# The clip of the scores in an integer softmax, moved from VectorE to GpSimd

## The chip, the cores and the metric

The kernel runs on one core of a Trainium2 chip. The metric is the device time of one execution in microseconds. The engines of the core are TensorE (PE in the profile; PEld is its weight load), VectorE (DVE), ScalarE (ACT), GpSimd (POOL) and SyncE (SP), which here only issues DMAs.

## The reference

The reference is a tower of eight blocks over tokens of 192 features: a choice of 87 of 125 tokens in each of 32 samples, then attention and feed-forward blocks in turn. The change lies in one of them, the attention of the third layer. Its 12 heads have 16 features each; queries, keys and values are quantised to whole numbers between -128 and 127, and the softmax is done on whole numbers:

```python
attn = jnp.einsum('bhnd,bhmd->bhnm', q, k) * Dh ** (-0.5)
attn = fq_act(attn, s_attn)            # round(t / s), clipped to 8 bits
...
x_int = x / scale
x_int = x_int - jnp.max(x_int, axis=-1, keepdims=True)
x_int = jnp.maximum(x_int, n * x0_int)
q = jnp.floor(x_int / x0_int)
r = x_int - x0_int * q
z = r * (r + b_int) + c_int
exp_int = jnp.maximum(jnp.floor(z * jnp.exp2(n - q)), 0.0)
exp_sum = jnp.sum(exp_int, axis=-1, keepdims=True)
ratio = jnp.round(exp_sum / jnp.maximum(exp_int, 1.0))
big = jnp.floor(jnp.log2(ratio))       # and a correction; out = 2 ** -big
```

## The kernel before, in words

The stage is `log_int_stage`. The 32 samples are taken two at a time: 16 units, j = 0 to 15. A unit has 2 x 12 heads x 87 queries as rows, packed into 17 chunks of 128 partitions, each chunk with 87 keys. In SBUF a chunk has a pitch of 88 columns, so a tile is 128 x 1496. Each engine has its own written-out order, with semaphores that count units between them. All tiles of the stage (`raw`, `score`, `above`, `lift`, `e`, `share` and so on) exist once, so each engine also waits until a tile has been read before it writes it for the next unit.

The steps of one unit, with the lines that the profile shows:

- `scores` (TensorE, L2418, L2424): q times k into PSUM `ps`. The query blocks come by DMAs that SP issues (L2452) after `scores_done` of an earlier unit.
- `take` (ScalarE, L3306, L3307): `ps` to `raw`, int32, rounded. It waits for `cut` of the unit before, since `raw` exists once.
- `clip` (VectorE, L3380): `raw` to `score`, bf16, clipped to -128 to 127. It waits for `raw_ready` of its unit and `less_done` of the unit before.
- `find_top` (VectorE, L3385, L3387, L3390): the maximum of each row, in two halvings and a reduction, to `top`.
- `take_off_top` (TensorE, L3253, L3255): score minus top in PSUM `mid`, by an identity and a minus identity. It waits for `top_ready` and for `squared` of the unit before, since `mid` exists once; its end is `less_done`.
- `lift_up` (ScalarE, L3311): `mid` to `above`, bf16.
- `quotient` (VectorE, L3365): `above` to `lift`, bf16.
- `remainder` (TensorE, L3264), `powers` (ScalarE, L3330), `squares` (ScalarE, L3334, ends in `squared`).
- `exponential` (VectorE, L3357, `e` from `square` and `power`), `sum_up` (L3361), `divide` (L3369, L3371, L3373, `share` from `e` and the reciprocals).
- `lines` (ScalarE, L3326, from `share`), `exponents` (VectorE, L3394 `sure`, L3399 `classes`).
- `turn` (TensorE, L3272), `copy_turned` (ScalarE, L3319, L3321), `weigh` (TensorE, L2758), `store` (VectorE, L3403).

These are overlapped across units. In one round j, VectorE does exponential j, sum_up j, quotient j+1, divide j, clip j+2, find_top j+2, exponents j, store j-1. ScalarE does lift_up j+1, copy_turned j-1, lines j, powers j+1, squares j+1, take j+3. TensorE does take_off_top j+1, turn j-1, remainder j+1, weigh j-1, scores j+3. GpSimd does only the memsets at the start of the stage (L3227, L3228).

Of the kernel before, what the change touches and what calls it, by code (L numbers as in the profile page):

```python
# [16 lines left out]
ALU = mybir.AluOpType  # L17
# [57 lines left out]
def across(ap, axis, n):  # L75

    ap = ap.unsqueeze(axis)
    shape = list(ap.shape)
    shape[axis] = n
    return ap.broadcast_to(shape)  # L80
# [3096 lines left out]
def chunks_of(sb):  # L3177

    return sb[:].rearrange("r (n k) -> r n k", k=PITCH)


def log_int_stage(kit, QK, VB, out, con, heads):
# [6 lines left out]
    nc = kit.nc  # L3189
    s_qk, ninv_x0, bound, whole_x0, half_b, rest_c, sigma = (con[:, j:j + 1] for j in (0, 3, 11, 12, 13, 14, 4))  # L3190
    to_int = con[0:NT, 15:16]
    U = UNITS
# [3 lines left out]
    with kit.stage("log_int") as ctx:  # L3196
        blocks, filled = heads.of, heads.filled
        raw, power, line, sure = (kit.sb(ctx, n, [128, FLAT], I32) for n in ("raw", "power", "line", "sure"))
        square, e, share = (kit.sb(ctx, n, [128, FLAT]) for n in ("square", "e", "share"))
        score, above, lift, classes = (kit.sb(ctx, n, [128, FLAT], BF16) for n in ("score", "above", "lift", "classes"))  # L3200
# [23 lines left out]
        @block.gpsimd  # L3224
        def _(pool):
            for k, value in enumerate((2.0 ** 21, 128.0 * (LEAST + CLASS0))):
                nc.gpsimd.memset(bias[:, k:k + 1], value).then_inc(made, 1)  # L3227
            nc.gpsimd.memset(raw[:], -1024).then_inc(made, 1)  # L3228

        @block.sync  # L3230
        def _(sp):
# [118 lines left out]
        @block.vector  # L3350
        def _(dve):
            v = nc.vector

            def exponential(j):
                dve.wait_ge(squared, j + 1)
                dve.wait_ge(power_ready, j + 1)
                v.scalar_tensor_tensor(e[:], square[:], rest_c, power[:].bitcast(F32), ALU.add, ALU.mult).then_inc(e_ready, 1)  # L3357

            def sum_up(j):
                dve.wait_ge(e_ready, j + 1)  # L3360
                v.tensor_reduce(total[:], chunks_of(e)[:, :, 0:NT], AX.X, ALU.add).then_inc(summed, 1)  # L3361

            def quotient(j):
                dve.wait_ge(above_ready, j + 1)
                v.tensor_scalar(lift[:], above[:], ninv_x0, whole_x0, ALU.mult, ALU.add).then_inc(lift_ready, 1)  # L3365

            def divide(j):
                dve.wait_ge(summed, j + 1)
                v.tensor_scalar(total[:], total[:], 1.0, None, ALU.max).then_inc(floored, 1)  # L3369
                dve.wait_ge(floored, j + 1)  # L3370
                v.reciprocal(recip[:], total[:]).then_inc(recip_ready, 1)  # L3371
                dve.wait_ge(recip_ready, j + 1)
                v.scalar_tensor_tensor(chunks_of(share), chunks_of(e), NEAR, across(recip[:], 2, PITCH), ALU.mult,  # L3373
                                       ALU.mult).then_inc(share_ready, 1)

            def clip(j):
                dve.wait_ge(raw_ready, j + 1)
                if j >= 1:
                    dve.wait_ge(less_done, j)
                v.tensor_scalar(score[:], raw[:], -128.0, 127.0, ALU.max, ALU.min).then_inc(cut, 1)  # L3380

            def find_top(j):
                dve.wait_ge(cut, j + 1)
                of = chunks_of(score)
                v.tensor_tensor(half[:], of[:, :, 0:PITCH // 2], of[:, :, PITCH // 2:PITCH], ALU.max).then_inc(halved, 1)  # L3385
                dve.wait_ge(halved, j + 1)
                v.tensor_tensor(quarter[:], half[:, :, 0:PITCH // 4], half[:, :, PITCH // 4:PITCH // 2],  # L3387
                                ALU.max).then_inc(quartered, 1)
                dve.wait_ge(quartered, j + 1)
                v.tensor_reduce(top[:], quarter[:], AX.X, ALU.max).then_inc(top_ready, 1)  # L3390

            def exponents(j):
                dve.wait_ge(line_ready, j + 1)
                v.tensor_tensor(sure[:], share[:].bitcast(I32), line[:], ALU.add).then_inc(sure_ready, 1)  # L3394
                dve.wait_ge(sure_ready, j + 1)
                if j >= 1:
                    dve.wait_ge(turned_done, j)
                high = sure[:].bitcast(I16).rearrange("r (w half) -> r w half", half=2)[:, :, 1]
                v.tensor_scalar(classes[:], high, -1.0 / 128.0, 254.75 - 1.0 / 256.0, ALU.mult, ALU.add).then_inc(class_ready, 1)  # L3399

            def store(j):
                dve.wait_ge(weighed, j + 1)
                v.tensor_scalar(out[:, 2 * j:2 * j + 2, :], p_out[:, :, 0:D], to_int, MAGIC, ALU.mult, ALU.add).then_inc(stored, 1)  # L3403

            v.memset(ps[:], 0.0).then_inc(cleared, 1)
            v.tensor_scalar(minus[:], kit.identb[:], -1.0, None, ALU.mult).then_inc(cleared, 1)
            v.tensor_scalar(times_x0[:], kit.identb[:], sigma, None, ALU.mult).then_inc(cleared, 1)
            for j in range(-AHEAD, U + 1):
                if has(j):
                    exponential(j)  # L3410
                    sum_up(j)
                if has(j + 1):
                    quotient(j + 1)
                if has(j):
                    divide(j)
                if has(j + 2):
                    clip(j + 2)
                    find_top(j + 2)
                if has(j):
                    exponents(j)  # L3420
                if has(j - 1):
                    store(j - 1)
# [231 lines left out]
def l2_attn(kit, H, stats, early, loads):  # L3654
    nc, dram = kit.nc, kit.dram
    W3 = 3 * D
    with ExitStack() as outer:
# [7 lines left out]

        CX = sb("cx", [NT, NB, D])
        log_int_stage(kit, QKB, VB, CX, con, heads)
        with ExitStack() as last:
            CT = sb("cT", [KP, HALVES, TOKENS], BF16, last)
# [127 lines left out]
```

## Time and profile before

| | |
|---|---|
| median of 3 runs | 2383.24 us (2379.29 to 2392.43) |
| time of the profiled execution | 2381.72 us |
| its span | 2379.3 us |
| busy in the span: PE, DVE, ACT, POOL | 1676.9, 1323.9, 1044.3, 344.1 us |
| the stage, from the first clip to the last store | 1431 to 1635 us |
| mean granted clock of TensorE, as a share of full speed | 0.83 |

The profile is one execution. Times in its rows are us from the start of the span unless they are marked ns. A row of the timeline has a start, a duration, engine, line, operation, written tile, read tiles, sizes, and in brackets the idle time of the engine before it with what ended it. Consecutive instructions of one form can be merged in one row ("x2").

### The profile page before, as it was taken

The numbers are of one execution on the slowest core, as the hardware profiler recorded it, in microseconds if no ns is written. First come the engines' busy times: TensorE is split into PE (matmuls) and PEld (weight loads), VectorE is DVE, ScalarE is ACT, GpSimd is POOL, SyncE is SP. The second block draws the span as 40 slices with busy tenths as digits, with TensorE's granted clock in tenths as the row PEclk, the third lists the DMA queues.
The fourth block names the chain that finished last, engine by engine and source line by source line (L and its number), as shares of the span: only waits on it lengthen the run. The fifth ranks groups of instructions, "written<-read, shape, count | busy, mean of one in ns | idle before, by whom it ended". The sixth has DMA issues, their size and how long they took to land. (4 is left out here: it accounts for less than half of the span.)

```text
span 2379.3 us, 35751 instructions
## 1 busy us (share of the span) xinstructions
PE 1676.9 (70%) x12022; PEld 1359.0 (57%) x12038; DVE 1323.9 (56%) x2732; ACT 1044.3 (44%) x2115; POOL 344.1 (14%) x417
## 2 busy tenths in 40 slices
PE   3588879947751377656589686664793699469995
PEld 2266658636641244336579563443683598369995
DVE  6599962350147989978712467997326211542223
ACT  4477742302224678876112147884322254312221
POOL 0000000006630000001043100000000342034431
PEclk9799969877875588987689896775897699679998
DMA  3200010304440000000467300000003453446775
GB/s 85 69 19 18 21 26 4 83 24 136 138 157 1 4 6 6 5 1 2 124 215 215 125 4 8 7 4 1 13 1 109 141 181 116 138 133 223 225 215 190
DMA packets 137245, 189.81 MB, mean 80 GB/s; under 512 B 51661, under 2 KB 111214, under 8 KB 137070
## 3 DMA queue, kind: packets, MB, share of 16 engines
q1 hardware_dynamic: 116289, 146.91, 20.2%
q0 software_dynamic: 15360, 36.72, 5.3%
q10 hardware_dynamic: 5420, 3.91, 0.6%
q8 instruction: 102, 1.67, 0.3%
q14 instruction: 74, 0.60, 0.1%
HBM read 150.21 MB, written 33.68 MB: 77 GB/s over the span
## 5 line engine op out<-in xcount | busy, mean ns | idle before, releaser
L989 DVE TENSOR_TENSOR 36_l3f_mlp_hidden<-36_l3f_mlp_gate,36_l3f_mlp_first 128x512 f32<-128x512 f32 x51 | 35.1, 688 | 185.3 <-ACT 36_l3f_mlp_gate L967 104.6
L882 PE MATMUL 36_l3f_mlp_first<-36_l3f_mlp_xT,36_l3f_mlp_w 128*128 128x128 f32 x816 | 101.5, 278 | 1.9 <-issue 1.9
L1005 DVE TENSOR_SCALAR 9_l0f_mlp_y<-9_l0f_mlp_second,l0f_routing_weight 128x192 f32<-128x192 f32 x51 | 20.4, 416 | 142.7 <-PE 9_l0f_mlp_second L896 63.1
L882 PEld LDWEIGHTS 36_l3f_mlp_first<-36_l3f_mlp_xT,36_l3f_mlp_w 128*128 128x128 f32 x816 | 97.0, 195 | 1.6 <-issue 1.6
L1245 PE MATMUL 2_performer_p_u<-perf_proj,2_performer_yT 128*87 128x512 f32 (+1 forms) x204 | 88.8, 577 | 10.6 <-DVE 2_performer_arg L1406 9.4
L967 ACT ACTIVATE 36_l3f_mlp_gate<-36_l3f_mlp_first 128x512 f32<-128x512 f32 x51 | 30.5, 598 | 137.5 <-PE 36_l3f_mlp_first L887 128.3
L1003 DVE TENSOR_TENSOR 32_l3a_mlp_y<-32_l3a_mlp_second,l3a_experts_b_rows 128x192 f32<-128x192 f32 x29 | 10.4, 358 | 136.8 <-issue 102.2
L896 PE MATMUL 36_l3f_mlp_second<-l3f_experts_w,36_l3f_mlp_hidden 128*128 x408 | 80.9, 342 | 0.0
L989 DVE TENSOR_TENSOR 22_l1f_mlp_hidden<-22_l1f_mlp_gate,22_l1f_mlp_first 128x512 f32<-128x512 f32 x29 | 20.0, 688 | 106.4 <-ACT 22_l1f_mlp_gate L967 85.5
L963 ACT ACTIVATE 32_l3a_mlp_hidden<-32_l3a_mlp_first,l3a_experts_b_cols 128x128 f32<-128x128 f32 x174 | 48.3, 378 | 65.9 <-PE 32_l3a_mlp_first L887 51.7
L2573 ACT ACTIVATE l1a_p<-14_pla_f,l1a_recip 128x87 int16<-128x87 f32 x272 | 71.7, 356 | 4.9 <-DVE l1a_recip L2662 4.9
L2543 PE MATMUL 14_pla_line<-14_pla_low,ident 128*128 128x435 f32 x96 | 50.5, 673 | 29.9 <-ACT 14_pla_low L2593 27.6
L896 PE MATMUL 9_l0f_mlp_second<-l0f_experts_w,9_l0f_mlp_hidden 128*128 x204 | 55.4, 401 | 22.2 <-issue 12.2
L856 POOL DMA_INDIRECT l3f_results<-36_l3f_mlp_y,l3f_routing_put x51 | 50.3, 987 | 136.0 <-DVE 36_l3f_mlp_y L1005 136.0
L896 PEld LDWEIGHTS 36_l3f_mlp_second<-l3f_experts_w,36_l3f_mlp_hidden 128*128 128x128 f32 x408 | 65.9, 192 | 6.5 <-issue 0.5
L896 PE MATMUL 32_l3a_mlp_second<-l3a_experts_w,32_l3a_mlp_hidden 128*128 x348 | 66.0, 341 | 2.4 <-ACT 32_l3a_mlp_hidden L963 2.4
L2543 PE MATMUL 14_pla_line<-14_pla_mid,ident 128*128 128x435 f32 x96 | 41.1, 564 | 36.2 <-DVE 14_pla_mid L2628 36.2
L963 ACT ACTIVATE 9_l0f_mlp_hidden<-9_l0f_mlp_first,l0f_experts_b_cols 128x128 f32<-128x128 f32 x102 | 32.1, 364 | 76.5 <-PE 9_l0f_mlp_first L887 43.0
L1245 PEld LDWEIGHTS 2_performer_p_u<-perf_proj,2_performer_yT 128*87 128x87 f32 x204 | 31.8, 169 | 56.4 <-issue 53.8
L930 ACT ACT_TABLE_LOAD x4 | 5.1, 1283 | 133.1 <-PEq L605 92.9
L887 PE MATMUL 36_l3f_mlp_first<-36_l3f_mlp_xT,36_l3f_mlp_w 64*128 64x128 f32 x816 | 60.5, 287 | 0.8 <-issue 0.8
L896 PEld LDWEIGHTS 32_l3a_mlp_second<-l3a_experts_w,32_l3a_mlp_hidden 128*128 128x128 f32 x348 | 57.4, 194 | 6.1 <-issue 2.9
(910 smaller groups left out, 4950.3 us busy)
## 6 DMA issues: line engine op xcount, KB each, us to landing
36_l3f_mlp_w<-in_L_ffn_w_dram SPq DMA_DIRECT2D x51, 768.0 KB
22_l1f_mlp_w<-in_L_ffn_w_dram SPq DMA_DIRECT2D x29, 768.0 KB
32_l3a_mlp_w<-in_L_attn_W_dram SPq DMA_DIRECT2D x29, 576.0 KB
9_l0f_mlp_w<-in_L_ffn_down_w_dram SPq DMA_DIRECT2D x51, 192.0 KB
l3a_experts_w<-in_L_attn_W_dram SPq DMA_DIRECT2D x8, 576.0 KB
l1a_blocks<-l1a_qkb SPq DMA_DIRECT2D x192, 5.4 KB, 1.8
l1f_experts_w<-in_L_ffn_w_dram SPq DMA_DIRECT2D x8, 384.0 KB, 6.3
l2a_blocks<-l2a_qkb SPq DMA_DIRECT2D x192, 5.4 KB, 1.8
```

Of the source, the lines that this page charges most:

```text
L856: nc.gpsimd.indirect_dma_start(route.results, to(i), y[i % NY][:], None).then_inc(put[i % NY], 16)
L882: nc.tensor.matmul(to(t + a * PAIRS), of[:, t + a * PAIRS, :], at[:, 0, :], start=(t == 0), stop=True, skip_group_check=True)
L887: ins = nc.tensor.matmul(to(t + a * PAIRS), of[rows, 2 * PAIRS + t, :], at[rows, 1, :], start=False, stop=True, skip_group_check=True)
L896: ins = nc.tensor.matmul(second[j % 2][:, 0:D], hidden[j % 2][:, t, :], ex.w2[:, ds(expert[j], 1), t, :].rearrange("p a w -> p (a w)"), st ...
L963: ins = nc.scalar.activation(out[:, t], src[:, t // PAIRS, t % PAIRS, :], func, bias=ex.b1_cols[:, ds(e, 1), t])
L967: nc.scalar.activation(out[:], src[:, 0, 0:HT, :], func).then_inc(done, 1)
L989: v.tensor_tensor(hidden[j % 2][:], gate[j % 2][:], first[j % 2][1][:, 0, 0:HT, :], ALU.mult).then_inc(hidden_done, 1)
L1003: ins = v.tensor_tensor(y[i % NY][:], of, ex.b2_rows[:, ds(e, 1), :].rearrange("p a w -> p (a w)"), ALU.add)
L1005: ins = v.tensor_scalar(y[i % NY][:], of, route.weight[:, i:i + 1], None, ALU.mult)
L1245: ins = t.matmul(p_u[:, k, 0:(EIGHT - h) * M], yT[b % 2][:, k, :], proj[:, h:EIGHT, :].rearrange("p h m -> p (h m)"), start=True, stop=True)
L2543: nc.tensor.matmul(to_w[:, n], kit.ident[:], of_w[:, n], start=start, stop=stop)
L2573: ins = a(P[:, j, n, :], f[j % 2][:, n * NT:(n + 1) * NT], ACT.Copy, scale=recip[:, j, n:n + 1])
```

## The change

The clip of each unit is issued by GpSimd, with the same two waits and the same semaphore, in a loop behind GpSimd's memsets. VectorE's `clip` and its call are taken out; its `find_top` waits for `cut` as before.

```diff
             nc.gpsimd.memset(raw[:], -1024).then_inc(made, 1)
+            for j in range(U):
+                pool.wait_ge(raw_ready, j + 1)
+                if j >= 1:
+                    pool.wait_ge(less_done, j)
+                nc.gpsimd.tensor_scalar(score[:], raw[:], -128.0, 127.0, ALU.max, ALU.min).then_inc(cut, 1)
...
-            def clip(j):
-                dve.wait_ge(raw_ready, j + 1)
-                if j >= 1:
-                    dve.wait_ge(less_done, j)
-                v.tensor_scalar(score[:], raw[:], -128.0, 127.0, ALU.max, ALU.min).then_inc(cut, 1)
-
             def find_top(j):
                 dve.wait_ge(cut, j + 1)
...
                 if has(j + 2):
-                    clip(j + 2)
                     find_top(j + 2)
```

## Rows read from the trace of the kernel before

**Rows 1.** Windows over the loop: length, busy us per engine, clock, DMA share, GB/s.
```profile
1465.40:1476.70 11.30, 7.83 (x76) 5.20 (x77) 11.06 (x14) 9.35 (x10) 0.00 (x0) 0.74 0.04 7
1431.00:1601.00 170.00, 109.01 (x1046) 72.27 (x1062) 159.20 (x183) 134.63 (x125) 0.00 (x0) 0.74 0.04 7
```

**Rows 2.** Groups of instructions, 1431 to 1601 us: busy us, mean ns, idle before.
```profile
L3380 DVE TENSOR_SCALAR 25_log_int_score<-25_log_int_raw 128x1496 bf16<-128x1496 int32 x15 | 14.0, 932 | 3.4 <-ACT 25_log_int_raw L3307 3.4
```

**Rows 3.** Timeline of one settled unit, 1522 to 1543 us.
```profile
1522.47 1.49 ACT L3334 ACTIVATE 25_log_int_square<-25_log_int_mid,l2a_con 128x1496 f32<-128x1496 f32 x1
...
1525.09 1.76 DVE L3357 SCALAR_TENSOR_TENSOR 25_log_int_e<-25_log_int_square,l2a_con,25_log_int_power 128x1496 f32<-128x1496 f32 x1
...
1526.80 1.51 ACT L3311 ACTIVATE 25_log_int_above<-25_log_int_mid,l2a_con 128x1496 bf16<-128x1496 f32 x1 [1.31 <-PE 25_log_int_mid L3255]
1526.88 1.70 DVE L3361 TENSOR_REDUCE 25_log_int_total<-25_log_int_e 128x17 f32<-128x1479 f32 x1
1528.49 0.66 DVE L3365 TENSOR_SCALAR 25_log_int_lift<-25_log_int_above,l2a_con 128x1496 bf16<-128x1496 bf16 x1
...
1531.21 0.93 DVE L3380 TENSOR_SCALAR 25_log_int_score<-25_log_int_raw 128x1496 bf16<-128x1496 int32 x1
1531.33 1.54 ACT L3326 ACTIVATE 25_log_int_line<-25_log_int_share,25_log_int_bias 128x1496 int32<-128x1496 f32 x1 [0.34 <-DVE 25_log_int_share L3373]
...
1532.18 0.55 DVE L3385 TENSOR_TENSOR 25_log_int_half<-25_log_int_score 128x748 bf16<-128x748 bf16 x1
...
1533.61 1.71 DVE L3394 CUSTOM_DVE_ANT_0 25_log_int_sure<-25_log_int_share,25_log_int_line 128x2992 uint16<-128x2992 uint16 x1
1534.11 1.49 ACT L3334 ACTIVATE 25_log_int_square<-25_log_int_mid,l2a_con 128x1496 f32<-128x1496 f32 x1
...
1542.86 0.93 DVE L3380 TENSOR_SCALAR 25_log_int_score<-25_log_int_raw 128x1496 bf16<-128x1496 int32 x1
```

**Rows 4.** A unit with a shorter step, and above's waits from 1454 to 1590 us.
```profile
1557.41 1.49 ACT L3334 ACTIVATE 25_log_int_square<-25_log_int_mid,l2a_con 128x1496 f32<-128x1496 f32 x1
1560.79 1.51 ACT L3311 ACTIVATE 25_log_int_above<-25_log_int_mid,l2a_con 128x1496 bf16<-128x1496 f32 x1 [0.35 <-PE 25_log_int_mid L3255]
...
ACT 25_log_int_above L3311 <- PE 25_log_int_mid L3255: 13.7, 12, 1.3
```

**Rows 5.** Timeline: the second lift, and the tail of the loop.
```profile
1447.11 0.67 DVE L3365 TENSOR_SCALAR 25_log_int_lift<-25_log_int_above,l2a_con 128x1496 bf16<-128x1496 bf16 x1 [0.85 <-ACT 25_log_int_above L3311]
...
1614.43 1.72 DVE L3394 CUSTOM_DVE_ANT_0 25_log_int_sure<-25_log_int_share,25_log_int_line 128x2992 uint16<-128x2992 uint16 x1 [1.61 <-ACT 25_log_int_line L3326]
```

**Rows 6.** GpSimd's work elsewhere: groups by form, then its wake-up in the timeline.
```profile
L3228 POOL MEMSET 25_log_int_raw<- 128x1496 int32 x1 | 1.4, 1356 | 0.0
L2977 POOL TENSOR_TENSOR H<-H,l1a_qb 128x1536 f32<-128x1536 f32 x1 | 3.4, 3409 | 6.8 <-issue 6.8
L336 POOL TENSOR_SCALAR_AFFINE_SELECT ident<-ident 128x128 f32<-128x128 f32 x1 | 0.3, 294 | 0.2 <-POOL 1_choose_place L332 0.2
L642 POOL MEMSET 21_l1f_dispatch_before<- 128x128 f32 x1 | 0.2, 210 | 31.8 <-POOLq L1668 31.8
...
1102.18 0.17 DVE L3039 TENSOR_REDUCE 19_l1a_close_m<-l1a_parts 87x1 f32<-87x16 f32 x1
1102.44 0.37 POOL L2974 PARTITION_ALL_REDUCE l1a_mx<-19_l1a_close_m  x1 [44.63 <-DVE 19_l1a_close_m L3039]
```

**Rows 7.** Timeline of an earlier stage, GpSimd and VectorE together, 1104 to 1116 us.
```profile
1104.77 0.36 DVE L3036 CAST 19_l1a_close_slot<-19_l1a_close_whole 87x768 bf16<-87x768 int16 x1
1109.61 3.41 POOL L2977 TENSOR_TENSOR H<-H,l1a_qb 128x1536 f32<-128x1536 f32 x1 [6.80 <-issue]
1109.70 3.54 DVE L3036 CAST 19_l1a_close_slot<-19_l1a_close_whole 87x768 bf16<-87x768 int16 x1
...
1113.88 0.40 DVE L3066 SCALAR_TENSOR_TENSOR H<-19_l1a_close_p_o,l1a_sc,H 128x192 f32<-128x192 f32 x1
...
1114.59 1.35 DVE L3036 CAST 19_l1a_close_slot<-19_l1a_close_whole 87x768 bf16<-87x768 int16 x1
```

## The prediction, made blind

> **What bounds the kernel now.** I first read the windows over the integer-softmax loop [rows 1]: from 1431 to 1601 us VectorE is busy for 159.20 of 170 us, ScalarE for 134.63, GpSimd for nothing. In the settled window of 11.3 us VectorE is busy for 11.06. So VectorE looks like the bound, and GpSimd like free room. The page's row of the clip says how much is to be moved [rows 2]: 15 clips in that window of 932 ns each, and the sixteenth like them.
>
> Then I read the timeline of one unit [rows 3], because a full engine and a full cycle of dependences can stand side by side. Clip to clip, VectorE takes 1542.86 - 1531.21 = 11.65 us, with no idle time before any of its instructions. That is the period. The cycle of dependences is this, each step read as a difference of starts in rows 3:
>
> - from the start of lift (L3365, 1528.49) through total, reciprocal and share to the start of line on ScalarE (1531.33): 2.84 us
> - line, power, up to the start of square (1534.11): 2.78 us, then square itself 1.49 us
> - from the end of square (1522.47 + 1.49 = 1523.96) over TensorE's subtraction of the top to the start of above (L3311, 1526.80): 2.84 us
> - above 1.51 us, and 0.03 us to the next lift.
>
> The sum is 11.49 us: the cycle is only 0.16 us shorter than VectorE's 11.65. The clip is not in it; find_top and its clip lie between share and exponents. The TensorE step is not always 2.84: [rows 4] show a unit with square at 1557.41 (ending at 1558.90) and above at 1560.79, which is 1.89 us. The wait of above for TensorE tells how often: in the slow unit above waits 1.31 us, in the fast one 0.35, and over 12 waits the total is 13.7 [rows 4], a mean of 1.14. So the mean cycle is 11.49 - 0.17 = 11.32 us.
>
> **What the change does to VectorE.** It loses the clip: half starts 0.97 us after the clip did (1532.18 - 1531.21). Part of that comes back at once, because sure needs line: before, sure starts 2.28 us after line (1533.61 - 1531.33); line itself lasts 1.54, and in the tail, where there is no clip and no find_top, sure waits for it (1.61 us of idle time at 1614.43) [rows 5]. So sure can't start sooner than some 1.57 us after line. VectorE's own floor becomes 11.65 - 0.71 = 10.94 us. The cycle of 11.32 is then longer, so even a free clip would bring 0.33 us a unit and not 0.97. Over the 12 settled periods, with 0.15 for the last, that is about 4 us. The gain is small whatever GpSimd does.
>
> **When the new clip runs.** Clip j+2 waits for less_done j+1 and for raw j+2. Raw comes first: take stands on ScalarE between square and above, and ScalarE has been idle for 1.31 us when above starts, so raw is there and less_done is the later one [rows 3]. GpSimd was woken 0.09 us after its producer in the nearest row (VectorE's reduction ends at 1102.35, the all-reduce starts at 1102.44) [rows 6]; above starts, as I estimate, 0.04 us after less_done. So the clip starts 0.05 us after above, and VectorE's e, the two-tensor instruction before it, ends at 1526.85, at the same moment. Find_top wants the clip only 1531.21 - 1526.85 = 4.4 us later. As long as the clip is shorter than that, nobody waits for its result: top, the next take (behind square) and the scores behind it are all earlier than they need to be. No DMA moves, SP's queue waits for scores_done as before, and nothing stands behind the clips on GpSimd in this stage.
>
> **The price that is not in the semaphores.** In an earlier stage the trace shows VectorE and GpSimd side by side [rows 7]. A cast of 87x768 int16 to bf16 that starts at 1109.70, just after GpSimd's addition started at 1109.61, lasts 3.54 us and ends 0.2 us after that addition's 3.41 us; the next one, at 1114.59, lasts 1.35 us and ends with the second addition; with GpSimd idle it takes 0.36 (at 1104.77). In between a VectorE instruction with one SBUF tensor and one in PSUM ran in 0.40 us (1113.88). So a cast is held for as long as GpSimd works, and that other form is not. Lift is a tensor-scalar from bf16 to bf16 in SBUF, 1496 elements in 0.66 us, more than two elements per ns, so it is of the cast's kind: I expect it to be held until the clip ends. The reduction sum_up before it takes 1.15 ns an element (1.70 us for 1479) and is not of that kind.
>
> The Trainium skill (SBUF — State Buffer, Who interferes with whom) states this as a rule: GpSimd and VectorE's second port pair are one exclusive lock, and copy, cast and tensor_scalar in a two-port mode or an instruction with two SBUF inputs waits for the whole instruction of the other. The trace agrees, with the cast of 3.54 us. By this rule lift waits; without it only the small gain above is left.
>
> If lift is held so, it starts not 1.54 us after above's start but 0.05 + T, T being GpSimd's time for the clip. The period becomes 11.32 - 1.54 + 0.05 + T = 9.83 + T as soon as T is above 1.49.
>
> **T.** No row has a GpSimd tensor-scalar of this size. From below: memset of raw, the same 1496 columns written and nothing read, 1.36 us. From above: the addition with two read tensors and one written, 3.41 us for 1536 columns, so 3.32 for 1496 [rows 6]. The clip reads one tensor and writes one. Half of the extra for two reads gives 1.36 + (3.32 - 1.36)/2 = 2.34 us, which I take; conversion from int32 and two operations speak for more, and affine_select, one read and one write, at 0.294 us against 0.211 for a memset of the same 128 columns, speaks for less. I keep 1.36 and 3.32 as ends.
>
> The Trainium skill (GPSIMD Engine Reference, Elementwise — side-by-side cycle accounting) has one-input bodies of at most two operations at 1.03 cycles per element, which would be an estimate of 1.28 us and some overhead. No run here shows it; by it lift is hardly held. It belongs to the first rival.
>
> **The sum for T = 2.34.** Lift 0 comes later by the longer clip 0, 2.34 - 0.93 = 1.41 us, and by its own hold, 0.05 + 2.34 - 1.54 = 0.85 us. The next two periods are cycle-bound already (lift waits for above, 0.85 us at 1447.11 and a little once more) [rows 5], and take 0.85 each. Then 12 periods up to lift 14 grow from 11.65 to 12.17, 12 x 0.52 = 6.3 us. The last period has no clip and loses 0.15. The sum is 1.41 + 0.85 + 1.70 + 6.3 - 0.15 = +10.1 us, and it goes by 16 us for each us of T (clip 0 and 15 holds). The stages after it only start later. The profiled execution took 2381.72 us, 1.5 us under the median of 2383.24, so the forecast is 2381.7 + 10.1 = **2392 us**. Half a per cent, 12 us, is about what a measurement of this kernel can tell from no change; the sum reaches it at T = 2.45 and is nought at T = 1.71.
>
> **Rivals.** (a) *The clip is short or lift isn't held.* At T = 1.36 lift is never held; clip 0 costs 0.43, the 12 periods shrink by 0.33 and the last by 0.15: -3.7 us, **2378 us**. The small select speaks for it; the 3.54 us cast speaks against lift running free. (b) *GpSimd is as slow as in its addition*, T = 3.32: 10.1 + 16 x 0.98 = +25.8 us, **2408 us**. It decides the sign from T = 2.45 on. Int32 in, bf16 out and two operations speak for it, one read against it. (c) *The small clip brings TensorE's step to its fast form as well*: with the 1.89 us in each unit the cycle is 10.54, VectorE's 10.94 the bound, 12 x 0.71 and 0.95 in each of the first two periods, about -10 us, **2371 us**. Nothing in the change makes TensorE busier before that step, since the idle time before it stays.
>
> **How the numbers follow.** The forecast (T from 1.7 to 2.7) 0.42; (a), with all T below 1.7, 0.22; (b), with all T above 2.7, 0.33; (c) 0.03. Of the forecast 0.08 lies beyond T = 2.45. Same is then 0.34 + 0.22 + 0.02 of (c) = 0.58, slower 0.33 + 0.08 = 0.41, and faster, which only an extreme (c) would reach, 0.01. The range goes from (a), with 2 us for the 1.5 between execution and median, 2376, to (b) and a little beyond for a T above the addition's, 2412.
>
> **What the profile after would show.** The clip as a GpSimd row of x16, its mean T; lift starting with idle time before it or lasting T instead of 0.66 us (how the cast of 3.54 showed it); above starting as before after less_done, 0.05 us before the clip; clip to clip 9.83 + T; half starting with share's end and sure waiting for line. Lift at 0.66 us and without idle time before it, with a T of 2 us or more, would make the hold wrong; periods under 11.2 us the cycle; a find_top that waits for the clip would mean T above 4.4 us. A first clip late by several us would be code that GpSimd has to load, which I don't count.

## The result, and the profile after

The changed kernel takes 2440.38 us (median of 4, 2437.67 to 2446.36) against 2387.84 us for the kernel before in the same comparison: a ratio of 1.023, 95% interval 1.0204 to 1.0257. It is slower by 2.3%; 2392 us with a range up to 2412 had been forecast. The profiled execution took 2437.82 us, 56.1 us more than the 2381.72 of before.

The groups of instructions of the changed kernel, from 1431 to 1660 us; the first answers to [rows 2], the second to the lift in [rows 3]:

```profile
L3233 POOL TENSOR_SCALAR 25_log_int_score<-25_log_int_raw 128x1496 bf16<-128x1496 int32 x16 | 83.8, 5236 | 144.1 <-PE 25_log_int_mid L3260 139.6 <-ACT 25_log_int_raw L3312 4.5
L3370 DVE TENSOR_SCALAR 25_log_int_lift<-25_log_int_above,l2a_con 128x1496 bf16<-128x1496 bf16 x15 | 63.2, 4213 | 11.5 <-ACT 25_log_int_above L3316 11.5
```

GpSimd's clip takes T = 5.24 us where VectorE's took 0.93, and lift, which nobody touched, lasts 4.21 us in place of 0.66. The windows of the changed kernel, one period of 15 us (columns as in [rows 1]), show VectorE busy for 13.77 us of it. A busy VectorE that does less work than before is the trap in this view: the busy time contains the hold.

```profile
1465.40:1480.40 15.00, 9.54 (x76) 6.50 (x77) 13.77 (x12) 9.62 (x10) 5.23 (x1) 0.64 0.03 5
```

The timeline of the changed kernel shows one period from above to above, the answer to [rows 3]:

```profile
1529.04 1.51 ACT L3316 ACTIVATE 25_log_int_above<-25_log_int_mid,l2a_con 128x1496 bf16<-128x1496 f32 x1 [1.31 <-PE 25_log_int_mid L3260]
1529.16 5.23 POOL L3233 TENSOR_SCALAR 25_log_int_score<-25_log_int_raw 128x1496 bf16<-128x1496 int32 x1 [9.81 <-PE 25_log_int_mid L3260]
1530.58 4.21 DVE L3370 TENSOR_SCALAR 25_log_int_lift<-25_log_int_above,l2a_con 128x1496 bf16<-128x1496 bf16 x1 [0.46 <-ACT 25_log_int_above L3316]
...
1534.71 0.16 DVE L3374 TENSOR_SCALAR 25_log_int_total<-25_log_int_total 128x17 f32<-128x17 f32 x1
...
1535.20 1.72 DVE L3378 SCALAR_TENSOR_TENSOR 25_log_int_share<-25_log_int_e,25_log_int_recip 128x1496 f32<-128x1496 f32 x1
...
1536.84 0.54 DVE L3384 TENSOR_TENSOR 25_log_int_half<-25_log_int_score 128x748 bf16<-128x748 bf16 x1
1536.96 1.54 ACT L3331 ACTIVATE 25_log_int_line<-25_log_int_share,25_log_int_bias 128x1496 int32<-128x1496 f32 x1 [3.74 <-DVE 25_log_int_share L3378]
...
1538.53 1.72 DVE L3393 CUSTOM_DVE_ANT_0 25_log_int_sure<-25_log_int_share,25_log_int_line 128x2992 uint16<-128x2992 uint16 x1 [0.18 <-ACT 25_log_int_line L3331]
...
1544.08 1.51 ACT L3316 ACTIVATE 25_log_int_above<-25_log_int_mid,l2a_con 128x1496 bf16<-128x1496 f32 x1 [1.31 <-PE 25_log_int_mid L3260]
```

The period is 1544.08 - 1529.04 = 15.04 us. The clip starts 0.12 us after above, lift starts when above is done, and ends 0.40 us after the clip (1534.79 against 1534.39). From there all is as in [rows 3]: lift's end to line 2.2 us, line to the next above 7.1. Half starts at share's end without a wait: the clip's result had been there for 2.45 us. So, behind the first unit, nobody waits for what GpSimd computes, only for GpSimd to be done. The waits of the changed kernel from 1470 to 1640 us (us in total, times, longest) say the same from the side of those who wait for lift and share:

```profile
PE 25_log_int_mid L3269 <- DVE 25_log_int_lift L3370: 47.4, 11, 4.8
ACT 25_log_int_line L3331 <- DVE 25_log_int_share L3378: 43.4, 11, 4.2
ACT 25_log_int_above L3316 <- PE 25_log_int_mid L3260: 15.7, 12, 1.3
```

### The profile page after: what moved, and what is told of

The parts are those of the page before. It is cut to its first block and busy times, and to the rows that moved or that the text cites. A ratio compares the mean times of both kernels' runs of the same rounds, so it can differ in the third digit from the quotient of the medians.

```text
span 2435.9 us, 35751 instructions
## 1 busy us (share of the span) xinstructions
PE 1707.3 (70%) x12022; PEld 1380.9 (57%) x12038; DVE 1362.4 (56%) x2716; ACT 1044.0 (43%) x2115; POOL 428.0 (18%) x433
## 5 line engine op out<-in xcount | busy, mean ns | idle before, releaser
L989 DVE TENSOR_TENSOR 36_l3f_mlp_hidden<-36_l3f_mlp_gate,36_l3f_mlp_first 128x512 f32<-128x512 f32 x51 | 35.1, 688 | 185.7 <-ACT 36_l3f_mlp_gate L967 103.8
L3233 POOL TENSOR_SCALAR 25_log_int_score<-25_log_int_raw 128x1496 bf16<-128x1496 int32 x16 | 83.8, 5236 | 144.1 <-PE 25_log_int_mid L3260 139.6
L3370 DVE TENSOR_SCALAR 25_log_int_lift<-25_log_int_above,l2a_con 128x1496 bf16<-128x1496 bf16 x16 | 63.9, 3992 | 12.0 <-ACT 25_log_int_above L3316 12.0
L3269 PE MATMUL 25_log_int_mid<-25_log_int_above,identb 128*128 128x512 bf16 (+1 forms) x47 | 22.5, 611 | 68.1 <-DVE 25_log_int_lift L3370 67.9
```

The source lines that it names most:

```text
L989: v.tensor_tensor(hidden[j % 2][:], gate[j % 2][:], first[j % 2][1][:, 0, 0:HT, :], ALU.mult).then_inc(hidden_done, 1)
L3233: nc.gpsimd.tensor_scalar(score[:], raw[:], -128.0, 127.0, ALU.max, ALU.min).then_inc(cut, 1)
L3269: ins = nc.tensor.matmul(flat[:, at], by[:], of[:, at], start=(k == 0), stop=(k == 1), skip_group_check=True)
```

## The experiments

Two theories stood against each other. H: the clip's length acts only by the hold of VectorE, as the prediction's sum has it. R: the chain waits for a result that comes late. T is the mean duration of GpSimd's instruction in the stage. Each run's stage is also measured in its own profile, from the start of the first take to the start of the last store (before: 1429.28 to 1634.14, 204.9 us). These lengths are free of what the other stages do from run to run, but are one execution each. e4 and e8 have a stage of their own ahead of the loop and are read only for what happens in it.

| run | T, us | stage, us | against before | ratio of times (95%) |
|---|---|---|---|---|
| the change | 5.24 | 260.4 | +55.6 | 1.023 (1.0204 to 1.0257) |
| e1 idle twin | 5.29 | 258.5 | +53.7 | 1.0234 (1.0217 to 1.0251) |
| e2 half | 2.74 | 211.7 | +6.9 | 1.0049 (1.003 to 1.0068) |
| e3 pieces | 2.78, 1.40, 2.69, 1.68 | 240.0 | +35.1 | 1.0156 (1.0139 to 1.0173) |
| e5 cast | 1.43 | 200.7 | -4.2 | 0.9974 (0.9958 to 0.9989) |
| e6 max only | 3.98 | 238.7 | +33.8 | 1.0138 (1.0104 to 1.0172) |
| e7 saturate | 1.44 | 200.1 | -4.8 | 0.9984 (0.9966 to 1.0002) |
| e9 min first | 1.44 | 200.9 | -3.9 | 0.9992 (0.9979 to 1.0005) |
| e10 fast twin | 1.58 | 206.0 | +1.1 | 1.0014 (1.0001 to 1.0027) |

**e1, the idle twin.** On the kernel before, VectorE's clip stays and GpSimd does the same clip into a tile `spare` that nobody reads. The main lines of the edit (the new tile, its semaphore and the rest are left out here):

```diff
+            for j in range(U):
+                pool.wait_ge(raw_ready, j + 1)
+                if j >= 1:
+                    pool.wait_ge(less_done, j)
+                nc.gpsimd.tensor_scalar(spare[:], raw[:], -128.0, 127.0, ALU.max, ALU.min).then_inc(spared, 1)
+            pool.wait_ge(spared, U)
...
                     act.wait_ge(cut, j)
+                    act.wait_ge(spared, j)
```

> The kernel before, with VectorE's clip kept, and beside it the same clip on GpSimd into a spare tile that nobody reads; only the next take and the end of the stage wait for it. Theory H (lift is held while GpSimd works): the twin costs as much as the change did, since the clip is not in the cycle: lift lasts about 4.2 us, clip to clip 9.83 + 5.23 = 15.06 us, in all some 2 to 3 us less than the changed kernel because unit 0 does not wait for it twice: +51 to +56 us over before. Rival R (the changed kernel is slow because find_top and what follows wait for a late result): nobody waits here, so within 0.3% of before.

Measured: 2438.26 us against 2384.15, a ratio of 1.0234. A timeline row pair of this run:

```profile
1530.65 5.23 POOL L3235 TENSOR_SCALAR 25_log_int_spare<-25_log_int_raw 128x1496 bf16<-128x1496 int32 x1 [9.81 <-PE 25_log_int_mid L3263]
1532.22 4.06 DVE L3374 TENSOR_SCALAR 25_log_int_lift<-25_log_int_above,l2a_con 128x1496 bf16<-128x1496 bf16 x1
```

GpSimd's result is used by nobody, VectorE still does its own clip, and nearly the whole loss is there: +53.7 us in the stage where the change has +55.6. The only instruction that waits for the twin is the next take, and it had to wait once, 6.21 us in the second unit; the settled period is 15.04 us, as in the change. R is out as the cause of this loss, and so is any story in which VectorE's clip matters to it: it rides along outside the cycle, as the prediction had it.

**e2, half.** The changed kernel, in which GpSimd clips the first 704 columns and VectorE the other 792; `cut` counts 2 a unit. The main lines of the edit:

```diff
-                nc.gpsimd.tensor_scalar(score[:], raw[:], -128.0, 127.0, ALU.max, ALU.min).then_inc(cut, 1)
+                nc.gpsimd.tensor_scalar(score[:, 0:704], raw[:, 0:704], -128.0, 127.0, ALU.max, ALU.min).then_inc(cut, 1)
...
+                v.tensor_scalar(score[:, 704:FLAT], raw[:, 704:FLAT], -128.0, 127.0, ALU.max, ALU.min).then_inc(cut, 1)
```

> The changed kernel with the clip cut in two: GpSimd does 704 of the 1496 columns, VectorE the other 792 where its clip was. If GpSimd's time goes by columns, T is 2.5 to 2.7 us. H: lift is held for 0.05 + T - 1.54 = 1.0 to 1.2 us, the period is 9.83 + T = 12.3 to 12.5 us, the whole +12 to +16 us over before (a ratio of 1.005 to 1.007). R: GpSimd is done 1.8 us before find_top wants it, so nothing is lost and VectorE's shorter clip brings up to 4 us: -4 to 0.

Measured: 2392.99 us, a ratio of 1.0049. Its interval, 1.003 to 1.0068 or 7 to 16 us, excludes R and not H's 12 to 16 us. The profile tells more: T is 2.74 us as H had it, but the stage is only 6.9 us longer, and the mean of the last 12 periods, from above to above, is (1613.91 - 1470.03) / 12 = 11.99 us and not 12.3 to 12.5. The timeline says why:

```profile
1530.17 2.71 POOL L3233 TENSOR_SCALAR 25_log_int_score<-25_log_int_raw 128x704 bf16<-128x704 int32 x1 [9.36 <-PE 25_log_int_mid L3260]
1531.60 0.67 DVE L3370 TENSOR_SCALAR 25_log_int_lift<-25_log_int_above,l2a_con 128x1496 bf16<-128x1496 bf16 x1
1532.18 0.74 DVE L3374 TENSOR_SCALAR 25_log_int_total<-25_log_int_total 128x17 f32<-128x17 f32 x1
```

Lift passes in 0.67 us in the middle of GpSimd's clip, and the little total after it, 0.17 us by itself, is held until GpSimd's end at 1532.88. "As long as GpSimd works" is therefore too simple for this instruction: the hold costs 0.57 us here and not 1.2.

**e3, pieces.** The changed kernel with GpSimd's clip as four instructions, columns 0, 352, 704, 1056 to 1496; `cut` counts 4 a unit.

> The changed kernel with GpSimd's clip cut into four instructions of 352, 352, 352 and 440 columns, 1.3 to 1.6 us each. H with a hold that ends with each instruction: lift waits for one piece only (about 1.2 us); total and share may each wait for another one: a period between 12.5 and 15.5 us, +20 to +60 us over before, with lift well under 4.2 us. If the hold lasts until GpSimd has nothing more queued: lift at 4.2 us or more and at least the +56 of the change. R (only the result's time counts): four fixed parts more, a little slower than the changed kernel.

Measured: 2420.78 us, a ratio of 1.0156. The timeline of this run:

```profile
1537.83 3.14 POOL L3233 TENSOR_SCALAR 25_log_int_score<-25_log_int_raw 128x352 bf16<-128x352 int32 x1 [4.46 <-PE 25_log_int_mid L3263]
1537.97 1.76 DVE L3365 SCALAR_TENSOR_TENSOR 25_log_int_e<-25_log_int_square,l2a_con,25_log_int_power 128x1496 f32<-128x1496 f32 x1
...
1541.38 0.66 DVE L3373 TENSOR_SCALAR 25_log_int_lift<-25_log_int_above,l2a_con 128x1496 bf16<-128x1496 bf16 x1
...
1542.45 1.72 DVE L3381 SCALAR_TENSOR_TENSOR 25_log_int_share<-25_log_int_e,25_log_int_recip 128x1496 f32<-128x1496 f32 x1
1542.53 2.88 POOL L3235 TENSOR_SCALAR 25_log_int_score<-25_log_int_raw 128x352 bf16<-128x352 int32 x1
1545.49 1.68 POOL L3236 TENSOR_SCALAR 25_log_int_score<-25_log_int_raw 128x440 bf16<-128x440 int32 x1
1547.20 0.55 DVE L3387 TENSOR_TENSOR 25_log_int_half<-25_log_int_score 128x748 bf16<-128x748 bf16 x1 [3.03 <-POOL 25_log_int_score L3236]
```

The hold of lift is gone, and the loss has moved: now GpSimd is the one that is held, its first and third piece lasting 3.14 and 2.88 us in place of 1.4 beside VectorE's two-tensor instructions e and share. The first piece had even started 0.14 us ahead of e, and e still took its usual 1.76 us. The result comes late, and half waits 3.03 us for it, a loss of the kind that R describes. The expectation named only VectorE's waits; the 37 us (2420.78 against 2384.15) fell in its 20 to 60 by luck, by another way.

**e4, prices.** The kernel before, with a stage of its own ahead of the loop in which single instructions are timed: GpSimd's forms with VectorE idle, then VectorE's forms each under one long GpSimd instruction. One execution.

> The kernel before with a stage of its own ahead of the loop, in which GpSimd runs 13 forms one by one with VectorE idle, and then 8 pairs: a long GpSimd instruction (6 times the clip, then twice a memset of 1496 columns) and under it one VectorE form. Theory C (the 5.23 us are the conversion from int32 and to bf16): float32 to float32 takes 1.5 to 2.5 us, int32 to bf16 5.2. Rival F (GpSimd's tensor-scalar is slow in itself, some 3.4 ns a column): all dtypes take 5 us, and one operation in place of two much less if the operations count. Pairs, by H: under the clip a bf16 tensor-scalar and a tensor-tensor from SBUF last until GpSimd ends; a reduction, a memset and the forms with a PSUM input take their own time; under a GpSimd memset the tensor-scalar is held and the tensor-tensor is not.

GpSimd's forms, each alone (timeline of this run; L3674 is maximum then minimum, L3675 the maximum alone, L3676 the first on 748 columns, L3677, L3678, L3681 to L3683 maximum then minimum again, L3679 multiply then add, L3680 multiply alone, L3684 and L3685 copies):

```profile
1448.47 5.29 POOL L3674 TENSOR_SCALAR 25_price_c<-25_price_i 128x1496 bf16<-128x1496 int32 x1 [72.31 <-DVE 25_price_acc L3701]
1453.84 3.98 POOL L3675 TENSOR_SCALAR 25_price_c<-25_price_i 128x1496 bf16<-128x1496 int32 x1
1457.91 2.71 POOL L3676 TENSOR_SCALAR 25_price_c<-25_price_i 128x748 bf16<-128x748 int32 x1
1460.70 5.23 POOL L3677 TENSOR_SCALAR 25_price_c<-25_price_f 128x1496 bf16<-128x1496 f32 x1
1466.01 5.23 POOL L3678 TENSOR_SCALAR 25_price_g<-25_price_f 128x1496 f32<-128x1496 f32 x1
1471.33 1.44 POOL L3679 TENSOR_SCALAR 25_price_g<-25_price_f 128x1496 f32<-128x1496 f32 x1
1472.85 4.00 POOL L3680 TENSOR_SCALAR 25_price_g<-25_price_f 128x1496 f32<-128x1496 f32 x1
1476.93 5.24 POOL L3681 TENSOR_SCALAR 25_price_c<-25_price_b 128x1496 bf16<-128x1496 bf16 x1
...
1492.87 1.43 POOL L3684 CAST 25_price_c<-25_price_i 128x1496 bf16<-128x1496 int32 x1
...
1495.88 3.33 POOL L3686 TENSOR_TENSOR 25_price_g<-25_price_f,25_price_h 128x1496 f32<-128x1496 f32 x1
```

C is wrong: the dtype changes nothing, 5.23 to 5.29 us for float32, int32, int16 and bf16 alike. F is half right: maximum then minimum is slow whatever the dtype, but multiply-add and the copies run in 1.43 to 1.44 us, and one operation alone is not a fast form either (4.00).

Under a GpSimd clip of 5.23 us, VectorE's forms of 1496 columns lasted (same timeline): tensor-scalar bf16 5.03, tensor-tensor of two SBUF tensors 4.28, reduction 1.72, tensor-scalar from PSUM 1.72, tensor-tensor of PSUM and SBUF 1.72; under a memset of 1.35 us the tensor-scalar lasted 1.06 and the tensor-tensor 0.94. The expectation holds, but for one thing: the tensor-tensor ended at 1516.07, 0.41 us before GpSimd's end at 1516.48. With some 0.94 us of its own, as under the memset, it was let in about 1.35 us before that end.

**e5, cast.** The changed kernel with a plain cast in place of the clip; scores beyond 8 bits stay as they are.

```diff
-                nc.gpsimd.tensor_scalar(score[:], raw[:], -128.0, 127.0, ALU.max, ALU.min).then_inc(cut, 1)
+                nc.gpsimd.tensor_copy(score[:], raw[:]).then_inc(cut, 1)
```

> The changed kernel with GpSimd's clip replaced by a plain cast of raw to score (scores beyond 8 bits stay unclipped). The cast took 1.43 us alone in the run of prices. All waits and tiles stay, only T falls from 5.23 to 1.43. Theory H with the prediction's sum: T is under 1.49, so lift is not held, the period is the bare cycle of 11.2 to 11.4 us, and the whole 3 to 4 us under before (rival (a) of the prediction). A theory in which any reading GpSimd instruction on this place costs by itself (arbitration, wake-up, semaphores) expects 2 us or more over before.

Measured: 2380.7 us against 2384.16, a ratio of 0.9974 (0.9958 to 0.9989), some 6 us less (3 to 10); the stage -4.2 us. With the same waits and tiles and a T of 1.43 us the whole loss of 56 us is gone. The instruction is another one here; e9 keeps its form.

**e6, max only.** As e5, with `tensor_scalar(score[:], raw[:], -128.0, None, ALU.max)`; the minimum is left out.

> The changed kernel with one of the two operations of the clip left out (only the maximum with -128); 3.98 us alone in the run of prices. The prediction's sum at T = 3.98: +10.1 + 16 x 1.64 = +36 us over before, period 9.83 + 3.98 = 13.8 us, lift lasting about 2.95 us. If the hold depends on more than the time (as in the half clip, where lift went through and only total was held), the period is shorter and the sum too high.

Measured: a ratio of 1.0138, and +33.8 us in the stage for an expected 36. Lift lasts 2.96 us in the settled unit. The period is 13.78 us in some units (above at 1531.54 and 1545.32), and its mean over the last 12 is (1640.88 - 1476.67) / 12 = 13.68, for an expected 13.8.

**e7, saturate.** The changed kernel with `raw` as int8, its memset -128, and GpSimd casting int8 to bf16.

> The changed kernel with raw held as int8: ScalarE's conversion on writing does the saturation, and GpSimd only casts int8 to bf16. If the int8 cast takes 1.4 to 1.5 us like the int32 one: as the cast run, 3 to 4 us under before. If it is a slow form (3.5 ns a column or more) lift is held again: +10 us or more.

Measured: a ratio of 0.9984 (0.9966 to 1.0002), the stage -4.8 us. The int8 cast takes 1.44 us, as the int32 one.

**e8, probes.** The kernel before, with a stage ahead of the loop: more of GpSimd's forms alone, then long GpSimd instructions under each of which VectorE runs a train of short ones of 128x16 float32, the probes. One execution.

> The kernel before with a stage of its own ahead of the loop: nine GpSimd forms alone, then eight long GpSimd instructions, under each of which VectorE runs a train of instructions of 128x16 float32, one after the other, as probes of the port: one-input tensor-scalar under clips of 1496, 1056, 704 and 352 columns, under a cast and under a memset; two-input tensor-tensor under clips of 1496 and 704. If the hold is one lock for the whole instruction: in each case one probe lasts until GpSimd's end and none gets through. If it is held only while GpSimd's reads and writes are under way (as the lift that passed under the half clip suggests): under the short clips probes pass in the middle and one is held near the end, under 1496 columns nearly none passes, and the two-input probes are free before the one-input ones. Operations: if the slow ones are those with maximum and minimum, multiply with add takes 1.4 us in both orders and for int32, and anything with a maximum 4 us or more.

The forms alone, timeline of this run: multiply then add on int32 (L3679), maximum then multiply (L3681), minimum then maximum (L3682), add alone (L3683):

```profile
1434.12 1.44 POOL L3679 TENSOR_SCALAR 25_probe_c<-25_probe_i 128x1496 bf16<-128x1496 int32 x1 [68.31 <-DVE 25_probe_i L3697]
...
1437.17 5.29 POOL L3681 TENSOR_SCALAR 25_probe_c<-25_probe_i 128x1496 bf16<-128x1496 int32 x1
1442.54 1.43 POOL L3682 TENSOR_SCALAR 25_probe_c<-25_probe_i 128x1496 bf16<-128x1496 int32 x1
1444.05 4.01 POOL L3683 TENSOR_SCALAR 25_probe_c<-25_probe_i 128x1496 bf16<-128x1496 int32 x1
```

The expectation that any form with a maximum is slow was wrong. The same clip with the minimum first takes 1.43 us, with the maximum first 5.23.

The probes, read in windows of 0.25 us by how many of them lie in each, so that every time below is good to about 0.2 us: under the clip of 1496 columns (from 1457.77) one one-input probe is held up to 1461.7, 3.9 us, and then they pass, 1.3 us before GpSimd's end. Under 1056, 704 and 352 columns the first hold lasts about 1.0, 0.65 and 0.35 us, and probes pass in the middle; under 704 and 352 the count falls from 5 to 3 a window near the end, a second, shorter hold. Two-input probes under 1496 columns pass from 3.8 us on, hardly sooner than the others. Under the cast of 1496 columns, 1.43 us long, a probe is held for some 1.3 us, nearly to its end; under the memset the probes pass from the start. So the first expectation, one lock for the whole instruction, is wrong for the clips; the second is right for the short ones and half right for 1496 columns, where it had nearly no probe pass and the two-input ones free earlier. The windows at the turn under 1496 columns:

```profile
1461.00:1461.25 0.25, 0.25 (x1) 0.50 0.00 0
1461.25:1461.50 0.25, 0.25 (x1) 0.50 0.00 0
1461.50:1461.75 0.25, 0.25 (x2) 0.50 0.00 0
1461.75:1462.00 0.25, 0.25 (x5) 0.50 0.00 0
```

This fits e2: lift asked 1.43 us into a clip of 704 columns, after the first hold, and total, asking at 2.0 us, could have run into the second. The probes are of another form than lift, so this is likely and not shown. Under the clip of 1496 columns lift (and the bf16 form of e4) was held until GpSimd's end, although the probes passed before it.

**e9, min first.** The changed kernel, the same clip with its operations in the other order.

```diff
-                nc.gpsimd.tensor_scalar(score[:], raw[:], -128.0, 127.0, ALU.max, ALU.min).then_inc(cut, 1)
+                nc.gpsimd.tensor_scalar(score[:], raw[:], 127.0, -128.0, ALU.min, ALU.max).then_inc(cut, 1)
```

> The changed kernel with the two operations of GpSimd's clip in the other order: the minimum with 127 first, then the maximum with -128, which gives the same numbers. Alone this form took 1.43 us against 5.23. With the prediction's sum T = 1.43 is under 1.49: lift not held, period 11.2 to 11.4 us, 3 to 6 us under before, as the cast run. If the order only matters with GpSimd alone, the run falls back to the changed kernel's +55.

Measured: 2382.68 us against 2383.19, a ratio of 0.9992 (0.9979 to 1.0005). The timeline of this run:

```profile
1468.85 1.51 ACT L3316 ACTIVATE 25_log_int_above<-25_log_int_mid,l2a_con 128x1496 bf16<-128x1496 f32 x1 [0.92 <-PE 25_log_int_mid L3260]
...
1525.97 1.51 ACT L3316 ACTIVATE 25_log_int_above<-25_log_int_mid,l2a_con 128x1496 bf16<-128x1496 f32 x1 [1.31 <-PE 25_log_int_mid L3260]
1526.10 1.44 POOL L3233 TENSOR_SCALAR 25_log_int_score<-25_log_int_raw 128x1496 bf16<-128x1496 int32 x1 [10.07 <-PE 25_log_int_mid L3260]
1527.52 0.67 DVE L3370 TENSOR_SCALAR 25_log_int_lift<-25_log_int_above,l2a_con 128x1496 bf16<-128x1496 bf16 x1 [0.47 <-ACT 25_log_int_above L3316]
...
1531.93 1.72 DVE L3393 CUSTOM_DVE_ANT_0 25_log_int_sure<-25_log_int_share,25_log_int_line 128x2992 uint16<-128x2992 uint16 x1 [0.18 <-ACT 25_log_int_line L3331]
...
1605.61 1.51 ACT L3316 ACTIVATE 25_log_int_above<-25_log_int_mid,l2a_con 128x1496 bf16<-128x1496 f32 x1 [2.85 <-PE 25_log_int_mid L3260]
```

The 56 us are gone, and the stage is 3.9 us shorter than before. VectorE is idle for 0.47 us before lift and 0.18 before sure: it is no longer the bound, the cycle is. On the whole kernel the gain is not clear of zero; of the 3 to 6 us under before that were expected, the interval (-5 to +1 us) holds a part.

**e10, fast twin.** The idle twin of e1, with the minimum-first clip.

> The kernel before with VectorE's clip kept and the minimum-first clip beside it on GpSimd into a spare tile that nobody reads (the idle twin with T = 1.43 in place of 5.23). If only the length of the hold counts: lift is not held and the time is that of before, within 0.3%. If every GpSimd instruction that reads beside VectorE costs something of its own, 5 us or more over before. Against e9 it also shows what VectorE's clip itself is worth: 3 to 6 us.

Measured: a ratio of 1.0014 (1.0001 to 1.0027), the stage +1.1 us, lift at 0.66 us in the mean. A reading GpSimd instruction at this place costs little by itself: 0 to 6 us by the interval, 1.1 by the stage. Against e9 the stages differ by 5.0 us; most of that is VectorE's clip, the rest what the twin costs.

## Why the prediction was wrong

**The term that was mis-sized is T, GpSimd's time for the clip.** The prediction took 2.34 us and kept "1.36 and 3.32 as ends"; it measured 5.24. The prediction's own sum at the measured T is 10.1 + 16 x (5.24 - 2.34) = +56.5 us, and the profiled executions differ by 56.1. Its period at T = 5.23 is 9.83 + 5.23 = 15.06, and 15.04 was measured. Term by term, at T = 5.24, the sum has 4.3 us for clip 0, 3.8 for the first hold, 7.5 for the next two periods, 41.0 for the twelve and -0.15 for the last; the starts of above and of the last store give 4.4, 3.6, 7.0, 40.7 and -0.1. So no other term needed repair.

The hit on the period to 0.02 us is in part luck, though: two sizes inside the 9.83 are off and cancel. The prediction let lift end 0.66 us after the clip and the clip start 0.05 us after above; it was 0.40 and 0.12, which is 0.19 us less a period. And it took 0.17 us off the cycle for units in which TensorE's subtraction is short. In the changed kernel there are none: above waits 1.31 us in each settled period but one (1.26). The short step goes with the granted clock: before, it took 1.89 us at a granted clock of 0.82 (1558.90 to 1560.79) and 2.8 at 0.50, the lower level of 1.2 GHz (1524.00 to 1526.80); in the changed kernel it ran at 0.50 (1526.20 to 1529.04), and the mean over one period fell from 0.74 [rows 1] to 0.64 in the window shown above. A mean over the units before was not a mean over the units after.

**Where the bound came from.** The upper end was an addition of two tensors, taken as the worst of GpSimd's work because it reads twice. The runs show that the number of tensors read does not bound the time: the same addition on 1496 columns takes 3.33 us, as worked out, but a one-tensor form takes 1.43 or 5.23 by its operations and their order. An operation that no row shows had been bounded by rows of other operations. The affine_select row, which was said to speak for less, had nothing to say either.

The Trainium skill's rate (GPSIMD Engine Reference, Elementwise — side-by-side cycle accounting), 1.03 cycles per element for one-input bodies of at most two operations, an estimate of 1.28 us here, agrees roughly with the 1.43 of e9 and not with the 5.23 of the change, a body of as many operations.

**The steps that held.** The cycle as the second bound: with T at 1.43 the mean period of e9 is (1605.61 - 1468.85) / 12 = 11.40 us, read from the starts of above, where 11.32 had been worked out; and the stages of e5, e7 and e9 gain 3.9 to 4.8 us where rival (a) had 3.7. That the totals agree so well is in part luck: in e9 those twelve periods gain 3.0 us against before and not 4.0, and the period from the first above to the second, which the sum for (a) left out, gains 1.2 (8.14 against 9.33). A free clip does not bring 0.97 us a unit. The hold of lift, read from the casts in another stage [rows 7], was the mechanism; e1 shows it without the change. Sure waits 0.18 us for line, as said. The slope of 16 us for each us of T: e6 at 3.98 has 36.3 by the sum and 33.8 in the stage.

**The steps that did not.** "A find_top that waits for the clip would mean T above 4.4 us": T was above, and after unit 0 find_top did not wait. Share moves back with lift, and the time that find_top leaves for the clip grows with the hold. And a cast "is held for as long as GpSimd works" fits the long clip; for the half clip's T of 2.74 the sum gives 16.5 us where the stage has 6.9. Whether it would also be too high for a whole clip of such a length, where the forecast itself lay, is not shown: no run had a clip of 1496 columns that took between 1.6 and 3.98 us.

**The rivals.** (b) had the direction, with a mechanism that was right and a T that was not far enough. (a) is what e9 shows. (c) is not seen in any run as it was put, with the short step in every unit: in e9 above waits 1.31 us in most units and 0.85 to 0.92 in every third, and a wait as short as 0.37 comes once, in e7.

## What to carry to other kernels

Before work moves to GpSimd, time the very instruction, with its operations in both orders: here one clip took 1.43 us or 5.23 us. Then ask not who waits for its result but which VectorE instruction asks for SBUF while it runs; a held instruction shows as a long busy one, not as a wait. And a full engine is not the bound by its fullness: a cycle of dependences 3% shorter stood behind it, so that even the fast form brought 4 us in the stage of the 15 that 16 clips of 0.93 us had promised.

## What the runs showed of the hardware that was not expected

- GpSimd's tensor-scalar on 128x1496: minimum then maximum, multiply then add and add then multiply take 1.43 to 1.44 us; maximum then minimum 5.23 to 5.29, maximum then multiply 5.29, and maximum, multiply or add alone 3.98 to 4.01. The dtype makes no difference where it was varied (four input types for maximum then minimum, two for multiply then add). Why the order does is not shown.
- The hold is not one piece for the whole instruction when that is short: under 352, 704 and 1056 columns VectorE's probes pass after 0.35, 0.65 and about 1.0 us, under 1496 only after 3.9 of 5.23. The three short holds are 0.92 to 0.99 ns a column, the pace of the cast (1.43 us for 1496, 0.96 ns a column). The Trainium skill (SBUF — State Buffer, Who interferes with whom) says that the loser blocks for the other's whole instruction; under the long clip lift does, under the half clip it did not. That the hold follows GpSimd's reads and its last writes would fit the short clips, and was not tested; why the clip of 1496 columns holds for 3.9 us stays open.
- The hold goes both ways: pieces of 1.4 us on GpSimd lasted 3.14 and 2.88 us beside VectorE instructions with two SBUF tensors; the first of these (e) began 0.14 us after the piece and was not held.
